# Candidate product of a GRU step summed from two accumulators on VectorE, input products spread evenly over the steps

## The reference

```python
def step(h, inp):
    x_t, prop = inp
    comb = jnp.concatenate([x_t, h], axis=-1)
    z = jax.nn.sigmoid(comb @ Wz + bz)
    r = jax.nn.sigmoid(comb @ Wr + br)
    comb2 = jnp.concatenate([x_t, r * h], axis=-1)
    h_cand = jnp.tanh(comb2 @ Wh + bh)
    h_new = (1.0 - z) * h + z * h_cand
    h_next = jnp.where(prop, jnp.tanh(h_new @ Wp + bp), h_new)
    return (h_next, h_new)
```

## Time and profile before

| | |
|---|---|
| median of 3 runs | 1042.85 us (1042.57 to 1042.98) |
| profiled execution | span 1041.4 us |
| busy, of the span | PE 99%, DVE 83%, ACT 73% |
| matmuls | 21386 |

### The profile page before, as it was taken

One profiled execution on the slowest core, in us unless ns is written; L12 is line 12 of the kernel. 1 busy time (PEld: TensorE's weight loads), 2 busy tenths in 40 slices (PEclk: granted clock), 3 DMA queues, 4 the chain that ended last, 5 costly groups with the idle time before them and its releaser, 6 DMA issues.

```text
span 1041.4 us, 49306 instructions
## 1 busy us (share of the span) xinstructions
PE 1036.1 (99%) x21386; PEld 956.5 (92%) x21386; DVE 860.2 (83%) x2859; ACT 761.1 (73%) x1789; POOL 0.2 (0%) x4
## 2 busy tenths in 40 slices
PE   9999999999999999999999999999999999999998
PEld 4577999999999999999999999999999999999998
DVE  6978888888888898888988888888888887776665
ACT  6877777776777777767777777777777677665666
POOL 0000000000000000000000000000000000000000
PEclk9999999999999999999999999999999999999999
DMA  9312211101111001111011110011110100000001
GB/s 327 114 63 64 83 54 44 42 4 43 43 43 43 23 24 42 44 43 43 7 39 43 43 43 24 23 43 43 43 44 12 34 23 23 23 24 24 24 4 44
DMA packets 38488, 47.33 MB, mean 45 GB/s; under 512 B 2176, under 2 KB 34048, under 8 KB 37888
## 3 DMA queue, kind: packets, MB, share of 16 engines
q1 hardware_dynamic: 38000, 44.12, 12.6%
q10 hardware_dynamic: 272, 0.07, 0.0%
HBM read 27.40 MB, written 16.78 MB: 42 GB/s over the span
## 4 chain that ended last, share of the span: by engine, by line
PE 98%; DVE 1%; ACT 0%; issue 0%; DVEq 0%
PE acc L1323 41%; PE x_acc L1237 34%; PE acc L1331 14%; PE x_acc L1127 8%; PE x_acc L1258 1%; ACT gate L570 0%; PE acc L1251 0%; DVE gate L1020 0%; DVE q_full L1027 0%; DVE q_split L1009 0%; PE x_acc L1245 0%; DVE q_split L1025 0%; DVE sum_a L933 0%; DVE x_lo L873 0%; DVE gate L1038 0%
## 5 line engine op out<-in xcount | busy, mean ns | idle before, releaser
L1237 PE MATMUL x_acc<-x_hi,win_hi 128*128 128x256 f16 x1092 | 297.7, 273 | 0.0
L1237 PE MATMUL x_acc<-x_lo,win_hi 128*128 128x256 f16 x1092 | 297.6, 273 | 0.0
L1237 PE MATMUL x_acc<-x_hi,win_lo 128*128 128x256 f16 x1092 | 297.6, 273 | 0.0
L576 ACT ACTIVATE gate<-acc,unscale 128x128 f32<-128x128 f32 (+1 forms) x467 | 148.8, 368 | 103.8 <-PE acc L1323 102.2
L1323 PE MATMUL acc<-q_split,wrec_hi 128*128 128x64 f16 x5088 | 204.8, 193 | 0.1
L570 ACT ACTIVATE gate<-gate,unscale 128x128 f32<-128x128 f32 (+1 forms) x233 | 98.6, 444 | 136.3 <-DVE gate L1038 80.8
L1323 PE MATMUL acc<-h_split,wrec_lo 128*128 128x64 f16 x4096 | 180.2, 193 | 0.4 <-DVE h_split L1082 0.4
L1323 PEld LDWEIGHTS acc<-q_split,wrec_hi 128*128 128x128 f16 x5088 | 172.7, 98 | 0.4 <-DVE q_split L1009 0.4
L1331 PE MATMUL acc<-h_split,wrec_hi 128*128 128x128 f16 x2608 | 172.4, 219 | 0.2 <-DVE h_split L1009 0.2
L536 ACT ACTIVATE x_part<-x_acc,bias,part_unscale 128x256 f32<-128x256 f32 x312 | 155.1, 565 | 17.8 <-PE x_acc L1237 17.7
L1323 PEld LDWEIGHTS acc<-h_split,wrec_lo 128*128 128x128 f16 x4096 | 155.1, 98 | 5.4 <-issue 0.6
(11 more groups left out here) (144 smaller groups left out, 1435.7 us busy)
## 6 DMA issues: line engine op xcount, KB each, us to landing
out_dram<-x_blk SPq DMA_DIRECT2D x30, 512.0 KB, 3.2
x_blk<-x_dram SPq DMA_DIRECT2D x24, 512.0 KB, 4.0
x_blk<-x_dram SPq DMA_DIRECT2D x3, 1024.0 KB, 8.0
x_part<-wz_dram SPq DMA_DIRECT2D x4, 256.0 KB, 5.9
x_part<-wh_dram SPq DMA_DIRECT2D x4, 256.0 KB, 5.9
x_part<-wr_dram SPq DMA_DIRECT2D x1, 1024.0 KB, 10.2
x_part<-wz_dram SPq DMA_DIRECT2D x1, 1024.0 KB, 12.4
x_part<-wh_dram SPq DMA_DIRECT2D x1, 1024.0 KB, 15.4
```

Source lines behind the costliest of these rows:

```text
L576: nc.scalar.activation(gate[g][:, half, :], acc[g][:, half, :], func, scale=unscale[:, g:g + 1]).then_inc(gate_ready[g], 1)
L1237: mm = nc.tensor.matmul(in_halves(x_acc[bank][:])[:, j], weights[g][:, slot_w, k, j * P:(j + 1) * P], in_halves(values[m % 2][:, slot_x, : ...
```

## The change

In the 70 joint steps without a propagation (t from 16 to 108, s = 0, 1, 2, 4, 5, 6) C is made like R: `rec_both` takes the place of two `rec` calls (16 matmuls of 128 columns for 32 of 64), the seed of C covers both parts of its bank (128x512), DVE sums the two parts in halves, and the tanh reads the sums. In the same steps DVE no longer makes the state's high part from `new` and `keep`. It makes the full value alone, and ACT copies that into `h_split` as float16, in one instruction placed between the seeds of R and Z. DVE's sum with x stands ahead of the low part. The input products are counted singly: 30 in each step without a propagation. Up to 4 of them stand inside C (`WITHIN_C`), and fewer where their group ends sooner. The semaphore `kept_x_ready` is folded into `keep_ready`, which plays a part in the last step alone.

```diff
-AHEAD_OF_C = 4
+JOINT_CANDIDATE_AT = (0, 1, 2, 4, 5, 6)
+WITHIN_C = 4
...
-STAGES_AT = [((), (0, 1)), ((), (2, 3, 4)), ((), (5, 6)), ((7, 8), (9,)), ((), (10, 11, 12)), ((), (13, 14)), ((), (15, 16, 17)), ((18, 19), (20,))]
+SPREAD = (30, 30, 30, (24, 36), 30, 30, 30, (24, 36))
...
-    def stages_of(t):
+    def seven_fill_of(t):
 
         m, s = divmod(t, BLOCK)
-        return STAGES_AT[s] if m + 1 in SEVEN else ((), ())
+        if m + 1 not in SEVEN:
+            return 0, 0, 0
+        first, share = sum(max(of) if isinstance(of, tuple) else of for of in SPREAD[:s]), SPREAD[s]
+        return (first, first + share[0], first + share[1]) if isinstance(share, tuple) else (first, first, first + share)
+
+    def ended(begin, stop):
+        return range(begin // PER_GROUP, stop // PER_GROUP)
...
-        half_seed_scale = sb("half_seed_scale", [P, 2])
+        half_seed_scale = sb("half_seed_scale", [P, GATES])
...
+        def joint_candidate(t):
+
+            return joint(t) and t % BLOCK in JOINT_CANDIDATE_AT
...
+        def ahead_of_c(t):
+
+            begin = seven_fill_of(t)[0]
+            ahead = begin + (AHEAD_OF_C if joint_reset(t) else 0)
+            return ahead, min(ahead + WITHIN_C, begin - begin % PER_GROUP + PER_GROUP) if joint_candidate(t) else ahead
...
-            def squash_sums(g, summed, count, halves):
+            def squash_sums(g, func, summed, count, halves):
 
                 for n, half in enumerate(halves):
                     act.wait_ge(summed, count + n + 1)
-                    nc.scalar.activation(gate[g][:, half], gate[g][:, half], ACT.Sigmoid, scale=unscale[:, g:g + 1]).then_inc(gate_ready[g], 1)
+                    nc.scalar.activation(gate[g][:, half], gate[g][:, half], func, scale=unscale[:, g:g + 1]).then_inc(gate_ready[g], 1)
...
-                if g == Z and joint(t) or g == R and joint_reset(t):
+                if g == Z and joint(t) or g == R and joint_reset(t) or g == C and joint_candidate(t):
...
                 if joint(t):
-                    squash_sums(Z, update_summed, JOINT.index(t), WHOLE)
+                    squash_sums(Z, ACT.Sigmoid, update_summed, JOINT.index(t), WHOLE)
                 else:
                     squash(Z, ACT.Sigmoid, t, WHOLE)
                 if ahead:
                     seed(Z, t + 1)
-                if t < T - 1:
+                if joint_candidate(t):
+                    squash_sums(C, ACT.Tanh, candidate_summed, 2 * candidates_before(t), HALVES)
+                elif t < T - 1:
                     squash(C, ACT.Tanh, t, HALVES)
...
                     for g in (R, Z):
                         if g not in late:
                             seed(g, t + 1)
+                        if g == R and joint_candidate(t):
+                            act.wait_ge(h_new_ready, 2 * t + 2)
+                            nc.scalar.copy(h_split[:, :, 0, :], h_even_odd[t % 2][:]).then_inc(h_hi_ready, 2)
...
-                    for n in stages_last:
+                    for n in ended(seven_first, seven_last):
                         read_stage(m + 1, n)
...
-                    nc.vector.tensor_scalar(half_seed_scale[:], seed_scale[:, R:Z + 1], 0.5, None, ALU.mult).then_inc(half_seed_scale_ready, 1)
+                    nc.vector.tensor_scalar(half_seed_scale[:], seed_scale[:, R:C + 1], 0.5, None, ALU.mult).then_inc(half_seed_scale_ready, 1)
+
+                if joint_candidate(t):
+                    dve.wait_ge(product_done[C], t + 1)
+                    for half in HALVES:
+                        nc.vector.tensor_reduce(flat(gate[C][:, half]), acc_bank[C][:, :, half].rearrange("p n k b -> p (k b) n"), AX_X,
+                                                ALU.add).then_inc(candidate_summed, 1)
...
-                for n, half in enumerate(HALVES):
-                    dve.wait_ge(new_ready, 2 * t + n + 1)
-                    nc.vector.tensor_tensor(split[:, half, 0, :], new[:, half, :], keep[:, half, :], ALU.subtract).then_inc(hi, 1)
+                if not joint_candidate(t):
+                    for n, half in enumerate(HALVES):
+                        dve.wait_ge(new_ready, 2 * t + n + 1)
+                        nc.vector.tensor_tensor(split[:, half, 0, :], new[:, half, :], keep[:, half, :], ALU.subtract).then_inc(hi, 1)
                 for n, half in enumerate(HALVES):
                     dve.wait_ge(new_ready, 2 * t + n + 1)
                     nc.vector.tensor_tensor(h_out[:, half, :], new[:, half, :], keep[:, half, :], ALU.subtract).then_inc(h_new_ready, 1)
+                def add_result():
+                    dve.wait_ge(h_new_ready, 2 * t + 2)
+                    nc.vector.scalar_tensor_tensor(out=x_blk[m % RING][:, :, s, :], in0=h_out[:], scalar=h_unscale,
+                                                   in1=x_blk[m % RING][:, :, s, :], op0=ALU.mult, op1=ALU.add).then_inc(out_ready, 1)
+
+                if joint_candidate(t):
+                    add_result()
                 for n, half in enumerate(HALVES):
                     dve.wait_ge(hi, count + n + 1)
                     dve.wait_ge(h_new_ready, 2 * t + n + 1)
                     subtract_hi(h_out, split, half).then_inc(lo, 1)
-                nc.vector.scalar_tensor_tensor(out=x_blk[m % RING][:, :, s, :], in0=h_out[:], scalar=h_unscale,
-                                               in1=x_blk[m % RING][:, :, s, :], op0=ALU.mult, op1=ALU.add).then_inc(out_ready, 1)
+                if not joint_candidate(t):
+                    add_result()
...
-                for n in stages_of(t)[0] + stages_of(t)[1]:
+                for n in ended(seven_fill_of(t)[0], seven_fill_of(t)[2]):
...
+            def sevenths(m, begin, stop):
+
+                for n in range(begin // PER_GROUP, (stop + PER_GROUP - 1) // PER_GROUP):
+                    stage(m, n, max(begin - PER_GROUP * n, 0), min(stop - PER_GROUP * n, PER_GROUP))
+
+            def stage(m, n, begin, stop):
...
-                    rec_both(Z, range(KC)).then_inc(product_done[Z], 1)
-                    if joint_reset(t):
-                        stage(m + 1, (stages_first + stages_last)[0], stop=AHEAD_OF_C)
+                    rec_both(Z, h_split, range(KC)).then_inc(product_done[Z], 1)
+                    sevenths(m + 1, seven_first, ahead)
...
                 rec(C, wrec_lo, q_split, LOW, 0, into=into)
-                rec(C, wrec_hi, q_split, LOW, 0, into=into)
+                if not joint_candidate(t):
+                    rec(C, wrec_hi, q_split, LOW, 0, into=into)
                 pe.wait_ge(q_hi_ready, 2 * t + 2)
                 rec(C, wrec_lo, q_split, HIGH, 0, into=into)
-                rec(C, wrec_hi, q_split, HIGH, 0, into=into)
+                if not joint_candidate(t):
+                    rec(C, wrec_hi, q_split, HIGH, 0, into=into)
+                else:
+                    sevenths(m + 1, ahead, within)
                 if behind:
                     rec(Z, wrec_hi, h_split, HIGH[1:], 1).then_inc(product_done[Z], 1)
                 pe.wait_ge(q_lo_ready, 2 * t + 1)
-                if t < T - 1:
+                if joint_candidate(t):
+                    rec_both(C, q_split, LOW)
+                    pe.wait_ge(q_lo_ready, 2 * t + 2)
+                    rec_both(C, q_split, HIGH).then_inc(product_done[C], 1)
+                elif t < T - 1:
                     rec(C, wrec_hi, q_split, LOW, 1)
                     pe.wait_ge(q_lo_ready, 2 * t + 2)
                     rec(C, wrec_hi, q_split, HIGH, 1).then_inc(product_done[C], 1)
@@ -1414,8 +1467,7 @@
...
-                    for n in stages_first:
-                        stage(m + 1, n, AHEAD_OF_C if joint_reset(t) and n == stages_first[0] else 0)
+                    sevenths(m + 1, within, seven_middle)
...
-                for n in stages_last:
-                    stage(m + 1, n, AHEAD_OF_C if joint_reset(t) and n == (stages_first + stages_last)[0] else 0)
+                    sevenths(m + 1, within, seven_last)
```

More of the change, by code:

```diff
@@ L362, in gru_kernel @@
         p_hi_ready, p_lo_ready = sem("p_hi_ready"), sem("p_lo_ready")
-        out_ready, kept_x_ready = sem("out_ready"), sem("kept_x_ready")
+        out_ready = sem("out_ready")
         def propagates(t):
@@ L374, in joint_reset, with candidates_before @@
             return joint(t) and t % BLOCK in JOINT_RESET_AT
+        def joint_candidate(t):
+            return joint(t) and t % BLOCK in JOINT_CANDIDATE_AT
         def resets_before(t):
             return sum(joint_reset(step) for step in range(t))
+        def candidates_before(t):
+            return sum(joint_candidate(step) for step in range(t))
+        def ahead_of_c(t):
+            begin = seven_fill_of(t)[0]
+            ahead = begin + (AHEAD_OF_C if joint_reset(t) else 0)
+            return ahead, min(ahead + WITHIN_C, begin - begin % PER_GROUP + PER_GROUP) if joint_candidate(t) else ahead
         def props_before(t):
@@ L695, in _ @@
                 if joint_reset(t):
```

(17 more changed lines are left out.)

10 lines of the change are left out of this document (5 added, 5 removed).

## The result

The changed kernel takes 1161.38 us (median of 4 runs, 1158.69 to 1164.95) against 1042.91 for the kernel before on the same chip: ratio 1.1137, with a 95% interval of 1.112 to 1.1154. That is 118.5 us more; the prediction said 55, and 1098 us in all (1076 to 1114). The direction was right, and the size lies far above the range. The profiled execution has a span of 1162.1 us, where the one before had 1041.4.

A forecast was written before the change was run, and what follows sets the result against it. PE's own work bounded the kernel, the ring fitting with 0.15 us to spare. Ring waits 38.5, less PE's 3.1, plus seed of Z 6.9 and late sigmoids 5.3 and 7.8, gave 55.4 us more: 1098 us, range 1076 to 1114.

The forecast's parts named there:

- the paragraph on the even spread: Input products on PE: still 252 a block, so equal work; s = 0, 2, 5 get 6 more, s = 1, 4, 6 get 6 fewer.
- The clock: Rival, 2% chance: PE's clock falls in the waits, a fifth of joint steps at half rate add 103 us, about 1200.
- Rival 1: Experiments' rival, no chance given: sum of C and copy cost more than predicted; bank waits only replace time PE waits anyway.
- The ring term: State, reset gate, candidate, new state: this chain grows by 1.32 us, PE waits 0.55 us in each of 70 steps, 38.5 us.
- The seed of Z: On ACT behind the copy: PE waits 0.15 us more after s = 0, 1, 4, 5, in 46 steps, 6.9 us.
- ACT late at the reset sigmoid: Next step's sigmoid late by 0.44 us after s = 1 (5.3 us); after s = 6, 0.71 us for PE (7.8 us).
- What was called hidden: Sum with x runs while ACT copies; products inside C cover the low part, PE waiting up to 0.2 us where two stand.
- PE's gain: C's matmuls on PE: 16 of 128 columns replace 32 of 64, saving 45 ns a step, 3.1 us in 70 steps.

The follow-up runs named there:

- first experiment: The changed kernel with the even spread alone: no step sums its candidate, no copy on ScalarE; 1076.35 us, ratio 1.0322.
- third: The changed kernel with input products spread 24, 30, 30, (30, 42), 30, 30, 30, (24, 36), so s = 0 and 2 end on whole groups; 1105.07 us, ratio 1.0596.
- filler run: The changed kernel plus 28 matmuls of 128 columns that nothing reads, ahead of the last six input products where s = 0 and 2; 1139.01 us, ratio 1.092.
- run of five steps: The changed kernel with s = 0 and 2 ending on whole groups, no copy, low part before sum with x, C summed except at s = 0, four products within C; 1057.34 us.

## Why the prediction was right in direction and wrong in size

**The step that failed** is the paragraph on the even spread: "A block still has 252 input products, so PE's work is the same." The work is the same; what the sentence leaves out is that a product that begins a group needs an empty bank. It treated input products as filler that can stand anywhere. In steps with s = 0 and 2 the last 6 of 30 can't run before a read that is queued behind the new state. The prediction had itself put the copy and the seeds into ACT's queue, and did not ask which other instruction stood behind them. The spread costs 33.4 us alone (first experiment) and 56.3 on top of the sum and the copy (third).

**The clock.** This rival was given 2% and dismissed with a wait of about 0.5 us behind which the clock had held. The wait that came was four times as long. By the filler run it is worth 22.4 us, not the 103 of the rival: it strikes behind the bank waits, and behind 17 of the 25. It does not stand by itself, though, since without the early groups there is nothing for it to follow.

**The account** of the 118.5 us: 62.2 for the sum of C and the copy with a harmless spread, and 56.3 for the early groups. Of those, 22.4 are clock, and about 34 are idle time: 53.1 us of bank waits, less what PE then no longer waits for the state (33.4 us in 68 waits in the third experiment, 14.1 in 41 in the changed kernel, 19.3 less), which gives 33.8. The two pages agree: PE is idle for 81.6 us of the span in the changed kernel and for 48.2 in the third experiment. Rival 1 is right in that second half only.

**The ring term** (predicted 38.5) was there and somewhat smaller. In the block shown the six waits lose 1.16, 0.58, 0.44, 0.44, 0.58 and 0.44, 3.6 us, or 3.0 without the 0.65 of that kernel's own. The prediction had 6 x 0.55 = 3.3. In 70 steps that is 35 us. **The seed of Z** was to cost 0.15 us more after s = 0, 1, 4 and 5 (6.9 us in all). It is about 0.05: behind the waits where it strikes, the 24 matmuls of 64 columns take 0.91 us (first line of the block), and 0.86 where nothing waits. That makes some 2 us, so the two terms are 37 for 45. The copy took 0.405 us on average against 0.40 predicted (the 47 steps with an even t; the others are the same):

```profile
L756 ACT CAST h_split<-h_even 128x256 f16<-128x256 f32 x47 | 19.1, 405 | 21.5 <-DVE h_even L1118 21.5
```

**ACT late at the reset sigmoid** (predicted 13.1 us) held too: 9.3 us in 23 waits, and with 0.16 for each 13.0, in the two places named, s = 2 (0.30) and s = 7 (0.51).

**What was called hidden** was not quite: where two products stand in C, PE's weight load also waits for the low part of the gate product, 8.3 us in 33 waits in the changed kernel. The prediction saw up to 0.2 us there and held that the ring sets the end. PE itself loses less than the weight load's waits say. In the third experiment:

```profile
PEld acc L1376 <- DVE q_split L1035: 8.8, 36, 0.4
...
607.06 0.27 PE L1282 MATMUL x_acc<-x_hi,win_lo 128*128 128x256 f16 x1
607.29 1.07 PE L1376 MATMUL acc<-q_split,wrec_hi 128*128 128x128 f16 x16
```

The wide matmuls start 0.23 behind the last product in place of 0.11, and 35 such steps make about 4 us.

**The sum against the runs.** With whole groups the change costs 54.6 us where the sum had 55.4; with the third experiment's spread 62.2, of which some 12 x 0.65 = 8 are that spread's own. So for a kernel without the early groups the sum came out right, but in part by luck, since its terms offset each other: 37 for 45 on the ring and the seed, and against it 4 us for the low part and some 3 that are in no wait of the tables (37 + 13 + 4 - 3 = 51, where 54 were measured).

**PE's gain** of 3.1 us could never be told from noise; 45 ns a step was predicted and one pair of traces shows 29.

## What to carry to other kernels

Filler work is only filler if nothing that it needs is released by the chain it is to cover: before you move a piece, list its own waits (the bank, the buffer) and read what stands ahead of the releasing instruction in *that* engine's queue. A second queue can be late too, as DVE is in the run of five steps. Where a ring fits with 0.15 us to spare, what is added to it beyond the cover that filler work can really give is lost in every step. When PE's busy time rises with fewer matmuls, look at the granted clock behind the longest waits.

## What the runs showed of the hardware

The granted clock fell to half (0.50 between 550.3 and 553.5 us of the changed kernel) behind waits of PE of 2.0 to 2.3 us, in 17 cases of 23 (and not behind one of 2.85), while the kernel with waits of up to 1.8 us (the even spread alone) kept 1.00 throughout. Behind equal waits (2.17 us) it came out both ways, so these traces don't give a length from which it falls. The Trainium skill (TensorE: Matmul & The Clock Gate, What's actually happening) says that the throttled state is the default and activity releases it; the filler run agrees, with 1.00 over the run for 43 us more work and 22.4 us less time.
